# The shared expert first: starting an expert stage before the last block's norm and the router

## The reference, cut to what matters

```python
h = _layernorm(x) * (1 + cb) + sb
logits = xf @ router_w.T + router_b                 # xf: h as 2048 x 128
routing = softmax(logits)
sel_w, sel_idx = top_k(routing, 2)
sel_w = sel_w / sel_w.sum(-1)
comb = zeros(2048, 8).at[..., sel_idx].set(sel_w)
ffn = lambda w1, b1, w2, b2: gelu(xf @ w1.T + b1) @ w2.T + b2      # 128 -> 512 -> 128
out = ffn(shared) + sum(comb[:, e] * ffn(expert e) for e in range(8))
x = x + gb * out
```

## Time and profile before

| | |
|---|---|
| median of 3 runs | 677.3 us (677.08 to 679.79) |
| profiled execution | 679.79 us, span 678.0 us |
| busy in the span | TensorE 606.8 us (89%), VectorE 545.4 (80%), ScalarE 486.1 (72%), GpSimd 173.3 (26%) |
| chain that ended last | TensorE 62%, VectorE 26%, ScalarE 5%, issue 5%, DMA 1% |

### The profile page before, as it was taken

How to read it: one execution, slowest core, us unless ns; L and a number is a source line. 1 busy time by engine, 2 the same in 40 slices (tenths; PEclk the granted TensorE clock), 3 DMA queues, 4 the chain that set the end, 5 groups by cost and what they waited for, 6 DMA issues and landing times.

```text
span 678.0 us, 11084 instructions
## 1 busy us (share of the span) xinstructions
PE 606.8 (89%) x3284; PEld 441.1 (65%) x3284; DVE 545.4 (80%) x1345; ACT 486.1 (72%) x857; POOL 173.3 (26%) x147
## 2 busy tenths in 40 slices
PE   8788889888997899999999999782699899999996
PEld 5355556555545568888888887351385788888884
DVE  3667888888866658878888887756899689999997
ACT  4548999999553669999999998677635466666663
POOL 3422223332301415443554443310143000000000
PEclk9789999999996899999999999976699799999999
DMA  7000000000100120122202220000000042222201
GB/s 239 1 0 2 2 2 0 0 0 0 32 1 0 48 113 37 57 95 94 91 2 93 93 85 1 23 1 0 0 1 0 1 150 87 87 86 86 86 1 62
DMA packets 6651, 29.85 MB, mean 44 GB/s; under 512 B 887, under 2 KB 1024, under 8 KB 4417
## 3 DMA queue, kind: packets, MB, share of 16 engines
q1 hardware_dynamic: 6610, 29.37, 12.2%
HBM read 28.18 MB, written 1.19 MB: 43 GB/s over the span
## 4 chain that ended last, share of the span: by engine, by line
PE 62%; DVE 26%; issue 5%; ACT 5%; DMA 1%; SPq 0%; POOL 0%; DVEq 0%; ACTq 0%; POOLq 0%
PE PS L1127 16%; PE PS L1129 16%; PE PS L1128 16%; DVE STAT L802 8%; PE PS L1273 2%; DVE RA L822 2%; PE PS L1228 2%; DVE HN L656 2%; PE PS L1153 2%; DMA AR<-in_wmod 1%; DVE SU L828 1%; PE PS L1242 1%; DVE HN L652 1%; ACT RA L605 1%; DVE AR L1086 1%
## 5 line engine op out<-in xcount | busy, mean ns | idle before, releaser
L937 DVE TENSOR_TENSOR RA<-AR,RA 128x512 fp32r<-128x512 f32 x140 | 134.3, 983 | 29.1 <-ACT RA L509 28.4
L508 ACT ACTIVATE AR<-PS,BI 128x512 f32<-128x512 f32 x144 | 99.4, 691 | 26.2 <-PE PS L1129 16.6
L1127 PE MATMUL PS<-HH,WH 128*128 128x512 f32 x272 | 109.5, 403 | 0.1
L1129 PE MATMUL PS<-HL,WH 128*128 128x512 f32 x272 | 107.4, 395 | 0.0
L1128 PE MATMUL PS<-HH,WL 128*128 128x512 f32 x272 | 107.3, 395 | 0.0
L509 ACT ACTIVATE RA<-PS,BI 128x512 fp32r<-128x512 f32 x144 | 98.4, 683 | 0.0
L802 DVE CUSTOM_DVE_ANT_0 STAT<-PS,MQ 128x128 f32<-128x128 f32 (+1 forms) x256 | 76.3, 354 | 20.2 <-PE PS L1229 20.1
L1127 PE MATMUL PS<-RA,WH 128*128 128x512 f32 x208 | 82.4, 396 | 2.5 <-DVE RA L1093 2.1
L1129 PE MATMUL PS<-RA,WH 128*128 128x512 f32 x208 | 81.2, 391 | 0.0
L1128 PE MATMUL PS<-RA,WL 128*128 128x512 f32 x208 | 81.2, 390 | 0.0
L312 POOL TENSOR_TENSOR AR<-AR 128x512 f32<-128x512 f32 x32 | 51.2, 1601 | 111.9 <-DVE AR L756 111.9
(11 more groups left out here) (196 smaller groups left out, 1185.1 us busy)
## 6 DMA issues: line engine op xcount, KB each, us to landing
AR<-comb SPq DMA_DIRECT2D x16, 1024.0 KB, 4.6
WS<-in_w SPq DMA_DIRECT2D x9, 512.0 KB, 5.6
WS<-in_w SPq DMA_DIRECT2D x8, 384.0 KB, 3.1
M<-in_mats SPq DMA_DIRECT2D x1, 1384.0 KB, 12.2
X<-in_xT SPq DMA_DIRECT2D x4, 256.0 KB, 4.8
out_xT<-X SPq DMA_DIRECT2D x4, 256.0 KB, 2.1
AR<-in_wmod SPq DMA_DIRECT2D x1, 768.0 KB, 9.2
KM<-in_kmats SPq DMA_DIRECT2D x1, 162.5 KB
```

What stands on the lines that cost most here:

```text
L508: act.activation(G[:, c, :], PS[:, c, :], ACT.Gelu_apprx_tanh, bias=bias).then_inc(s["act"], 1)
L937: dve.tensor_tensor(out=GL[:, m0 % 2, c, :], in0=G[:, c, :], in1=f(GH[:, m0 % 2, c, :]), op=ALU.subtract).then_inc(s["lo"], 1)
L1127: pe.matmul(out, wh, xh, start=first, stop=False)
L1129: return pe.matmul(out, wh, xl, start=False, stop=last)
```

## The change

The shared expert becomes k = 0, so its four visits come first and need no gates. TensorE starts `hidden0(0, 0)` when block 0 alone has its lower part; `mean(1, 3)` follows two groups later, and three routers, the spread of the last root and the last router stand between the groups of steps 0 and 1. The last block's inverse root takes no Ln and Exp on ScalarE: the variance is summed with tokens on partitions (four narrow matmuls), ScalarE adds the epsilon (128 x 4, Identity), GpSimd raises it to -0.5 (`pow`), and TensorE spreads it over a bank. The route takes no Exp of the logits: it finds the two largest logits and GpSimd raises e to their difference (128 x 16, `pow`); its VectorE operations are given out in ones to threes between the lower parts of steps 1 to 4. The four unweighted outputs are copied to ACC (`keep0`), and the biases added later (`add_bias`). GpSimd no longer makes lower parts; it splits the second expert's weights before block 0, not after it. The loops of this stage are written out, and the hidden biases are read in place, without copies on ScalarE. The last visits are weighted: `residual_last` runs `scale0` first and adds from YW.

```diff
+            sp.wait_ge(s0["stored"], 16)
+            gates0(1)
+            gates0(2)
+            for k in range(3, E0):
+                weights0(k)
+                gates0(k)
...
+            def next_weights(k):
+                s = moe[0]
+                gp.wait_ge(s["w_in"], 16 * (k + 1))
+                if k >= 2:
+                    gp.wait_ge(s["y"], 4 * (k - 1))
+                split_weights(0, k, k % 2, 1024)
...
-            gp.wait_ge(moe[0]["w_in"], 16)
-            split_weights(0, 0, 0, 1024)
-            for t in range(NBLK):
+            next_weights(0)
+            next_weights(1)
+            for t in range(3):
                 split_hidden(1, HN, t)
-            for c in range(4):
...
-            gp.wait_ge(moe[0]["w_in"], 32)
-            split_weights(0, 1, 1, 1024)
-            experts(0, E0, 1024)
...
+            gp.wait_ge(ve_done, 1)
+            gp.tensor_tensor(out=RS[:, :], in0=VE[:, :], in1=CON[:, 3:4].to_broadcast([128, 4]), op=ALU.pow)\
+              .then_inc(root_done, 1)
+            split_hidden(1, HN, 3)
+            gp.wait_ge(moe[0]["rstep"], 11)
+            gp.tensor_tensor(out=ODDS[:, :], in0=CON[:, 4:5].to_broadcast([128, 16]), in1=RM["den"][:, :], op=ALU.pow)\
+              .then_inc(odds_done, 1)
+            next_weights(2)
+            gp.wait_ge(moe[0]["acc_init"], 4)
+            acc(4)
+            acc(5)
+            for k in range(3, E0):
+                next_weights(k)
+                for m in range(4 * k - 6, 4 * k - 2):
...
+                act.wait_ge(var_done, norm_at(1, 3) + 1)
+                act.activation(VE[:, :], PS[:, variance_bank(1, 3), 0:4], ACT.Identity, bias=CON[:, 0:1])\
+                   .then_inc(ve_done, 1)
+            def gelu0(m, c):
...
+            gelu0(0, 0)
...
-            inverse(1, 3)
...
-            def gelus(m, m0, e):
+            gelu0(0, 2)
+            biased_variance()
+            gelu0(0, 3)
...
-                   .then_inc(nrm_done, 1)
+                if (k, t) == (1, 3):
+                    dve.wait_ge(spread_done, 1)
+                    root = PS[:, variance_bank(1, 3), :]
+                else:
+                    dve.wait_ge(rstd_done, roots(k, t))
...
+            def scale0(m):
+                k, t = visits[m]
+                dve.wait_ge(moe[0]["y"], m + 1)
+                dve.wait_ge(moe[0][f"wb_in{(k - 1) % 2}"], 16 * ((k - 1) // 2 + 1))
+                if 6 <= m < 34:
...
+                dve.tensor_tensor(out=YW[:, m % 2, :], in0=PS[:, 4 + m % 4, :],
+                                  in1=WB[:, (k - 1) % 2, t * BLK:(t + 1) * BLK], op=ALU.mult)\
+                   .then_inc(moe[0]["ymul"], 1)
+            def residual_last(t):
+                m = visits.index((E0 - 1, t))
+                scale0(m)
...
+                dve.wait_ge(moe[0]["ymul"], m - 3)
                 for b in (2 * t, 2 * t + 1):
...
                                                    scalar=MG[:, 0, 1, b:b + 1], in1=blk(X, b, SEQ),
                                                    op0=ALU.mult, op1=ALU.add)
...
+            def second_chosen():
+                dve.wait_ge(s["rstep"], 10)
+                dve.tensor_reduce(km2, k2, axis=AX.X, op=ALU.max).then_inc(s["rstep"], 1)
+                dve.wait_ge(s["rstep"], 12)
+                dve.tensor_tensor(out=k2, in0=k2, in1=each(km2), op=ALU.is_equal).then_inc(s["rstep"], 1)
+            def shares():
+                dve.wait_ge(odds_done, 1)
+                dve.tensor_scalar(den, ODDS[:, :], 1.0, None, ALU.add).then_inc(s["rstep"], 1)
+                dve.wait_ge(s["rstep"], 14)
+                dve.reciprocal(m1, den).then_inc(s["rstep"], 1)
...
             normalise(1, 0)
             normalise(1, 1)
+            rest(1, HN, 0)
             attended(3)
+            rest(1, HN, 1)
             normalise(1, 2)
-            rest(1, HN, 0)
-            rest(1, HN, 1)
             centre(1, 3)
             rest(1, HN, 2)
-            normalise(1, 3)
-            rest(1, HN, 3)
...
+            def keep0(m):
+                t = visits[m][1]
+                dve.wait_ge(s["y"], m + 1)
+                dve.tensor_copy(blk(ACC, t), PS[:, 4 + m % 4, :]).then_inc(s["kept"], 1)
...
+            lower0(0)
+            lower0(1, (nothing, lambda: normalise(1, 3), lambda: rest(1, HN, 3), largest))
+            lower0(2, (first_equal, first_chosen, second_largest, second_equal))
+            lower0(3, (second_chosen, nothing, nothing, nothing))
+            keep0(0)
+            keep0(1)
+            lower0(4, (shares, weigh_chosen, combine, nothing))
+            keep0(2)
+            lower0(5, (nothing, lambda: keep0(3), lambda: rows_in(0), lambda: rows_in(1)))
+            lower0(6, (lambda: rows_in(2), lambda: rows_in(3), nothing, lambda: add_bias(0)))
+            lower0(7, (lambda: add_bias(1), nothing, nothing, lambda: add_bias(2)))
+            add_bias(3)
+            scale0(4)
+            for m in range(7, 32):
+                lower0(m + 1)
+                scale0(m - 2)
+            lower0(33)
+            scale0(30)
...
             residual_experts(1)
-            residual_shared(0)
-            lower0(35, 35, (lambda: residual_experts(2), lambda: centre(2, 0), lambda: residual_experts(3),
-                            lambda: residual_shared(1)))
+            residual_last(0)
+            lower0(35, (lambda: residual_experts(2), lambda: centre(2, 0), lambda: residual_experts(3),
+                        lambda: residual_last(1)))
...
                 pe.wait_ge(sq_done, at + 1)
+                if (k, t) == (1, 3):
+                    pe.wait_ge(cen_done, 8)
+                    for i in range(4):
+                        mm = pe.matmul(PS[:, 6, i:i + 1], STAT[:, BLK * t + 128 * i:BLK * t + 128 * i + 128],
+                                       OND[:, 0:1], start=True, stop=True)
...
-            router(0, 0)
-            router(0, 1)
-            mean(1, 3)
-            router(0, 2)
-            variance(1, 3)
-            router(0, 3)
...
+            def spread_root():
+                pe.wait_ge(root_done, 1)
+                for i in range(4):
+                    mm = pe.matmul(PS[:, 6, 128 * i:128 * i + 128], RS[:, i:i + 1].to_broadcast([128, 128]), IDF[:, :],
+                                   start=True, stop=True)
+                mm.then_inc(spread_done, 1)
...
+            def hidden0(m, c):
+                k, t = visits[m]
                 w = slice(128 * c, 128 * c + 128)
-                if m0 >= 1:
+                if m < 4:
+                    pe.wait_ge(hl_done, m + 1)
+                if m == 0 and c < 3:
+                    pe.wait_ge(cen_done, 4 + c + 1)
+                if m >= 1:
                     pe.wait_ge(s["act"], 2 * (4 * m - 3 + c))
...
+            def output0(m, c):
+                k, t = visits[m]
                 w = slice(512 + 128 * c, 640 + 128 * c)
                 pe.wait_ge(s["lo"], 4 * m + c + 1)
-                if c == 0 and m0 >= 4:
...
+                    if m == 0:
+                        pe.wait_ge(lnv_done, 7)
+                    elif m == 2:
+                        pe.wait_ge(nrm_done, 8)
+                    elif m == 3:
+                        pe.wait_ge(s["rstep"], 1)
+                    elif 4 <= m < 8:
+                        pe.wait_ge(s["kept"], m - 3)
+                        if m >= 6:
+                            pe.wait_ge(s["acc_init"], (1, 4)[m - 6])
+                    elif m >= 8:
+                        pe.wait_ge(s["ymul"], m - 7)
+                mm = three(PS[:, 4 + m % 4, :], WH[:, k % 2, w], WL[:, k % 2, w], GH[:, m % 2, c, :],
...
+            def routers_between(c):
+                if c == 0:
+                    pe.wait_ge(ot_done, UNITS)
+                    router(0, 0)
+                elif c == 1:
+                    variance(1, 3)
+                elif c == 2:
+                    router(0, 1)
+                else:
+                    router(0, 2)
+            def last_router_between(c):
+                if c == 0:
+                    spread_root()
+                elif c == 2:
+                    router(0, 3)
             def routes_between(c):
-                if c == 1 or c == 2:
-                    route_out(0, E0, 2 * c - 2)
-                    route_out(0, E0, 2 * c - 1)
+                if c < 2:
...
+                route_out(0, E0, c)
...
+                if c % 2 == 1:
+                    bias_out(2 + c // 2)
...
-            step0(32, 32, 8)
-            step0(33, 33, 8)
+                hidden0(0, c)
+                if c == 1:
+                    mean(1, 3)
+            step0(0, between=routers_between)
+            step0(1, between=last_router_between)
+            step0(2)
+            step0(3)
+            step0(4, between=routes_between)
+            step0(5, between=biases_between)
+            step0(6, between=last_biases_between)
```

(57 more changed lines are left out.)

326 lines of the change are left out of this document (138 added, 188 removed).

## The result

The changed kernel takes 681.72 us (median of 12 runs, 678.55 to 684.19), the kernel before 677.97 on the same chip (12 runs). The ratio is 1.0047, 95% interval 1.0025 to 1.007: 3.2 us slower (the two medians themselves lie 3.75 apart). The interval leaves out 1, so the change is slower, but by less than the 3.4 us that the prediction took as what can be told from no change; the time is inside its range of 672 to 683 us. The execution that was profiled is the shortest of the twelve (678.55 us, span 676.8), while the one shown of before is a long one (679.79). So the two traces alone would say that the change gains 1.2 us. What differs between executions had to be found too.

A forecast was written before the change was run, and what follows sets the result against it. TensorE bounds the stage's body; only the opening, with 13 us idle or at half clock, and the VectorE-bound end can move. Front -0.5 plus end +2.3 gives +1.8 us: 679.1 us from the median 677.3, range 672 to 683.

The forecast's parts named there:

- the two large terms of the sum: Opening of the first expert stage, 0.5 us gained; end of that stage, 2.3 us lost.
- The first of the prediction's own signs of being wrong: First expert stage: the forecast is wrong if steps 1 to 4 show no stand above 2 us.
- The other two: Signs of being wrong: a table load or long `pow` before 220 us; the tail's means keeping their distances.
- The pace and the walk to step 4: Opening: first group 204.2, first output group 209.9, step 1 ends 228.8, TensorE reaches step 4 at 241.1 us.
- Step 4: First expert stage: third keep waits for GpSimd's split until 245.5; TensorE stands 4.4 us, half clock adds 1.6.
- rival B: VectorE and GpSimd don't meet in step 4: stand 1.8, clock stays up, step 7 at 266, 674.7 us; chance 0.20.
- The front: Opening up to step 7's start: 270.4 us instead of 270.9, so 0.5 us gained.
- The transposes: TensorE in the opening: four sets at about 0.9 us, counted in its 54 us of work.
- The attention's split: Second weight split moved into attention's tail: VectorE can lose 2.3 once, covered by an output projection; 0, otherwise 0.5 us.
- `pow` and Identity: Opening: `pow` 0.1 to 1.3 us with over 5 of slack, taken as 0; Identity 0, or two loads of 1.28.
- the term of 2.3: Stage's end: `scale0` of 0.68 ahead of each `residual_last` makes the last mean 2.3 us later.
- The bound for the meeting: Stage's end: 3.5 us lost if third and fourth also meet GpSimd's split (up to 0.8) and half clock costs 0.4.

## Why the prediction was right, and where it was not

The time (679.1 forecast, 672 to 683 as the range) and the direction are right, but by luck: the two large terms of the sum were both too small and nearly cancel. The first of the prediction's own signs of being wrong did come, as steps 1 to 4 show no stand above 2 us (the longest is 1.45). The other two did not: ahead of 220 us there is only the Gelu table load that the walk has (207.11) and a power of 1.03, and the tail's means moved.

- **The pace and the walk to step 4: right.** With the variance as zero (1.81 later here), the first group was forecast at 204.2 and came at 204.27, the first output group 209.9 and 209.86, the end of step 1 228.8 and 228.6, TensorE's arrival in step 4 241.1 and 241.06. The stands in step 1 are 1.45 and 0.51, for 1.5, 0.4 and 0.85.
- **Step 4: the step that failed.** "Third keep at 245.5, so TensorE stands 4.4": it ended at 242.06 on that scale, close to the 242.4 that the working had for an undisturbed VectorE. The split starts when it was expected (239.87 for 239.9), but the working let two lower parts and the keep wait for all of it. Only one lower part fell beside its short first half, which cost 0.41; the keep reads PSUM and went through beside the second half (2.68), which hit the lower part after it. 1.84 us of stand instead of 4.4, and the clock stayed at 1.00. The numbers are those of rival B (0.20), step 7 at 265.95 for its 266, though not its condition: the two engines did meet. Where a wait is charged for a meeting of two engines, both instructions' starts have to be laid side by side, not their sums. The front gained 4.6 (3.5 by the other profile of before), not 0.5.
- **The transposes** are a smaller miss of the same sign: 0.61 a set of four, not 0.9.
- **The attention's split: the cover was not there.** Forecast 0, bound 0.5; measured 0.8 to 1.05, in six of the seven profiles with the split there (the seventh, the run without the scaling, lost nothing: 144.04). The argument rested on one small operation that waits; the one behind it, on two SBUF tiles, waits as well (2.56 for 0.43).
- **`pow` and Identity: right to be 0.** There is no table load ahead of the Identity. The power on 4 columns takes 1.03 us, that on 16 takes 3.27, outside the bound of 1.3 taken from wider additions; its slack hid it.
- **The end: the term of 2.3 was right, the meeting undersized.** Without GpSimd beside it it is 2.46 (0.80, 1.59, 1.87 and 2.46 at the four means, for 0.7, 1.4, 1.6 and 2.3). The bound for the meeting was 3.5 in all; 3.0 was measured in one execution and 6.0 in another. The bound counted the first half of the split only. An update in two halves can wait for both halves of the split, one after the other (1.15 and 2.02 for 0.48 each).
- **The sum.** Attention +0.8 to +1.05, opening -3.5 to -4.6, end +3.0 or +6.0: from -0.8 to +3.6, against a measured +3.2 (1.7 to 4.7). The profiled execution is one of the good ones. That the slow end is the commoner one is argued and not shown: the kernel without the scaling lies 6.2 us below the changed one, the kernel with the splits moved 2.5 to 3.2 us, which fits the 19.63 of the second profile (6.05 and 3.6) better than the 16.62 of the first (3.0 and 0.6). Of the four profiles with that end, two are of either kind (16.62 and 17.30; 19.63 and 20.21). The stretch from the fourth mean to the first mean behind the second layer's attention-like part varies too: 74.97 and 74.26 us in the two profiles of before, 73.41 in the first and 74.51 in the second of the changed kernel, and 75.82 without the scaling. The clock goes with most of that: over the 24 us from the fourth mean its mean is 0.86 and 0.93 in the two of before, 0.93 and 0.89 in the two of the changed kernel, 0.86 without the scaling. Why it falls more in some executions is open.

## What to carry to other kernels

A GpSimd operation on wide SBUF tiles is a hazard for every VectorE operation on two SBUF tiles, and in these rows also for one that reads and writes SBUF alone; an operation with an input in PSUM went through. The price is the rest of the GpSimd instruction, or of two. When an order is changed, lay both queues side by side at every such place, and send work of GpSimd's that isn't urgent (here weights split at 430 and first used at 526 us) to where VectorE's results are not awaited. A reordering that saves in an opening can lose it at an end that gets one more operation per block: four times 0.7 on the chain became 2.5 us, and with a meeting 3 to 6. And one profile is one throw: before explaining a difference of medians, profile the same kernel twice.

## What the runs showed of the hardware

- Two instructions that start 0.05 us apart on VectorE and GpSimd were resolved both ways in two executions of one kernel: 1.45 or 3.09 us for the same pair of updates. VectorE's row starts first in both.
- A VectorE operation with one input, in SBUF, waits for GpSimd's split as well: 0.64 for 0.18 (the cast at 184.33), and 2.69 for 0.73 (two operations of L694 at 436.47 in the first profile, beside the split at 435.80 and 437.21). One that reads PSUM doesn't: 0.68 at 243.19, in the middle of a subtraction of 2.68.
- The same split, one place later in GpSimd's queue, changed TensorE's stand in step 1 from 0.5 to 3.1 us, and the clock was at half behind it (0.75, 0.50, 0.50 in three stretches of 4 us): 5.2 us between the medians for 2.6 us more of stand.
- GpSimd's `pow` costs 1.03 us for 4 columns and 3.27 for 16, the latter more than twice an addition of 512 columns (1.3).
